# Linear attention and a gated scan: one product moved from GpSimd to VectorE, B and C's products in one piece, eight mask slots

## Chip, cores and metric

One NeuronCore of a Trainium2 chip. The metric is the device time of one execution in microseconds, the median of several runs.

## What is computed

The input `x` has 128 sequences of 64 steps and 256 features. Two blocks follow one another, in float32:

```
xn = layernorm(x);  q, k, v = xn @ Wq + bq, xn @ Wk + bk, xn @ Wv + bv    # 16 heads of 16
k, v masked;  q = softmax(q over a head), k = softmax(k over the steps)
y = q @ (k^T v) per head
x1 = x + silu(layernorm(y) * (1 + scale) + shift) @ film_out_W + b        # scale, shift from cond

h = (layernorm(x1) * (1 + scale) + shift)[:, perm]                        # scale, shift, gate from cond
xm, z = split(h @ W_in);  xm = silu(causal conv of 4 taps(xm) + conv_b)   # 512 channels
dtr, B, C = split(xm @ W_xp);  dt = softplus(dtr @ W_dt + b_dt)           # 64, 16, 16 columns
step: hst = hst * exp(dt * A) + (dt * x) B;  y = hst . C                  # 512 channels x 16 states
out = x1 + gate * ((y + xm * D) * silu(z)) @ W_out, put back by inverse perm
```

## The kernel before

**Attention** runs over 64 tiles of 128 rows (two sequences) in a software pipeline of 11 stages. Each engine goes through iterations j = 0 to 73 and does, in an order written out by hand, its part of every stage; tile k is in stage s at iteration k + s. Semaphores count tiles. SyncE's queue (lines 1115 to 1182) does in iteration j: `load(j+2)` of an input tile into ten slots, `load_mask(j+2)`, which spreads one row of the mask over 128 partitions into one of MRING = 4 slots `mneg`, then the store of the normalised `xh` of tile j-10 to DRAM, then the store of `x1` of tile j-7. `reuse(sp, S["k_biased"], k, MRING)` makes the mask load of tile k wait until VectorE has biased the keys of tile k - MRING (line 1607, which reads `mneg`). Everything in SyncE's queue is issued in order. GpSimd's iteration (line 1207) begins with `xh` of tile j-9, which waits until `xh` of tile j-11 is stored (two slots; SyncE issues that store in its iteration j-1), then scales `kT`, adds a bias to `xt`, computes three `rstd`, and normalises `yn`. TensorE turns `yn` (1337), then `xn` (1342), then projects (1352), and makes the keys (1370), which VectorE biases.

**The scan** goes over 16 chunks of T = 4 steps. The time is the batch's: a tile is 128 sequences at one step by 512 channels. A body of 64 items (one item is one of 16 states at one step) is written per chunk, `slot(c, i)` on each engine, with the side work of the next two chunks put into fixed slots (tables at lines 310 to 324: a position counts slots from the body of chunk k - 2). Per item:

- ScalarE makes four pieces of exp(dt A), `decay` (832), two pieces per slot, a block of eight items ahead;
- TensorE turns them into one of four PSUM banks (708), two slots ahead. It may do so once the item four before has been updated;
- VectorE multiplies the bank with the state, `keep_state` (970), and adds dt x times B, `feed_state` (980). It goes by pairs of items, `two_slots` (1011): two products, two updates;
- GpSimd or, for the items in ON_SCALAR, ScalarE scales the new state by C into one of eight slots (616, 878). For the ten items in PAIRED GpSimd also adds the scaled state of the item before to it (621), so that TensorE sums one in place of two;
- TensorE adds it up by transposing products (723), five slots later.

Side work per chunk: modulation of gathered rows on GpSimd, transposes `h`, input products `u` and `z` (two slots each), the taps of the convolution, whose last one ScalarE makes from its own SBUF copy `raw` (868) and whose other three GpSimd multiplies and adds (636, 640) in slots 46 to 69; `dtr`, then B and C's product `bcT` in two pieces of two column groups in slots 20 and 21 (775), their reduction `bc`, four `dt` products (785). ScalarE's softplus reads them twice, Relu and Abs (860, 861), then Exp (873) and one Ln (908, slot 36). GpSimd adds dt in slots 39, 41, 43, 45 (647) and multiplies it by x in slots 40, 42, 44, 46 (650). TensorE turns the products in slots 57, 59 and 66, 69 (789) and ScalarE copies them to `dtx`. Output products `out0` stand in slots 60, 61, 63, `out1` in slots 9 to 11 (753). For the first chunk VectorE does the sums and products itself (1078, 1081), and the pieces of a product stand back to back.

At the end a last stretch adds rows to the residual and stores them.

Of the kernel before, what the change touches and what calls it, by code (L numbers as in the profile page):

```python
# [25 lines left out]
P = 128  # L26
# [20 lines left out]
ON_SCALAR = (1, 3, 5, 16, 26, 36, 45, 47, 49, 51, 53, 55, 57, 59, 61, 63)  # L47
PAIRED = (7, 11, 13, 21, 23, 25, 29, 31, 33, 35)
RING = 8
# [3 lines left out]
AHEAD = 2  # L53
MRING = 4
STAGES = 11
# [9 lines left out]
def build(nc, x, cond, itok, mask, norm_scale, norm_bias, Wq, bq, Wk, bk, Wv, bv,  # L65
# [11 lines left out]
    with ExitStack() as ctx:  # L77
# [192 lines left out]
        s_tapadd = sem("conv_taps_added_gpsimd")  # L270
        s_tap0 = sem("conv_first_tap")
        s_xs, s_zs = sem("xs_ready"), sem("zs_ready")
# [33 lines left out]
        def at(start, *slots):  # L306
# [3 lines left out]
        SLOTS = {"dtr": at(B1, 13, 14), "out1": at(B3, 9, 10, 11), "dt0": at(B1, 18), "z0": at(B1, 16, 17),  # L310
                 "bcT": at(B1, 20, 21), "dt1": at(B1, 23), "bc": at(B1, 24, 25), "z1": at(B1, 28, 29),
                 "dt2": at(B1, 27), "z2": at(B1, 32, 33), "dt3": at(B1, 31), "z3": at(B1, 35, 36),
# [9 lines left out]
        MODULATE, CARRY, LN = at(0, 14, 18), B1 + 9, B1 + 36  # L322
        SOFTPLUS = at(B1, *range(39, 39 + 2 * CB))
        ROWS = {"out1": B3 + 12, "out0": B3 + 0}
# [259 lines left out]
        def mamba_gpsimd(gp):  # L584
# [39 lines left out]
            def add_tap(k, which, step):  # L624

                m, j = POOL_TAPS[which]
                if (m, j) not in taps_of(k):
                    return
                done = taps_to(k) + taps_of(k).index((m, j))
                x = xs[k % 2][:, m, :]  # L630
                if step == 0:
                    if j == 0:
                        gp.wait_ge(s_tap0, k * CB + m + 1)
                    reached(gp, s_tapadd, done)
                    apart(gp)
                    gp.tensor_scalar(tap[:, :], raw[:, m, j * P:j * P + TOK], taps[:, m, j:j + 1], 1.0,  # L636
                                     ALU.mult, ALU.mult).then_inc(s_tapmul, 1)
                else:
                    gp.wait_ge(s_tapmul, done + 1 - len(POOL_TAPS))
                    gp.tensor_tensor(x, x, tap[:, :], ALU.add).then_inc(s_tapadd, 1)  # L640

            def softplus_times_x(k, m, step):

                v = dtT[k % 2][:, m, :]
                if step == 0:
                    gp.wait_ge(s_softexp, softplus_steps(k + 1))
                    gp.tensor_tensor(v, v, tmp[:, m, :], ALU.add).then_inc(s_dt, 1)
                else:
                    gp.wait_ge(s_dt, k * CB + m + 1)
                    gp.tensor_tensor(tmp[:, m, :], v, xs[k % 2][:, m, :], ALU.mult).then_inc(s_dtxT, 1)  # L650

# [7 lines left out]
            def slot(c, i):  # L659

                if scanned(c) and i not in on_scalar_of(c):
                    scale_state(c, i)
                if scanned(c) and i - 1 in paired_of(c):
                    add_pair(c, i - 1)
                for n in range(STAGES_IN):
                    if c == CHUNKS - 1 and i == EARLY_SLOTS[n]:
                        add_early(n)
                for step, position in enumerate(POOL_TAP_SLOTS):
                    k = chunk_at(c, i, position)
                    if k is not None:  # L670
                        add_tap(k, step // 2, step % 2)
                k = chunk_at(c, i, CARRY)
                if k is not None:
                    carry(k)
                for step, position in enumerate(MODULATE):
                    k = chunk_at(c, i, position)
                    if k is not None:
                        modulate(k, step)
                for step, position in enumerate(SOFTPLUS):
                    k = chunk_at(c, i, position)  # L680
                    if k is not None:
                        softplus_times_x(k, step // 2, step % 2)

# [11 lines left out]
        def mamba_tensor(pe):  # L695
# [43 lines left out]
            def fill(k, job, piece):  # L739
# [33 lines left out]
                elif kind == "bcT":  # L773
                    for g in (2 * piece, 2 * piece + 1):
                        mm = pe.matmul(side[g * 2 * DS:(g + 1) * 2 * DS, :], w_xp[:, g, DTR:DTR + 2 * DS],
# [47 lines left out]
        def mamba_scalar(act):  # L823
# [11 lines left out]
            def move(k, job):  # L835
# [8 lines left out]
                elif kind == "u":  # L844
                    if k == 1:
                        act.wait_ge(s_carry0, b + 1)
                    elif b == 0:
                        act.wait_ge(s_carried, max(k, 1))
                    ins = act.activation(raw[:, b, (TAPS - 1) * P:], side[:, :], ACT.Copy)
                elif kind == "dtr":  # L850
# [6 lines left out]
                elif kind == "dt":  # L857
                    if b == 0:
                        reached(act, s_decay, (k - 1) * BLOCKS * GROUP * CB)
                    act.activation(dtT[k % 2][:, b, :], side[:, :], ACT.Relu, bias=dt_bias[:, b:b + 1])  # L860
                    ins = act.activation(tmp[:, b, :], side[:, :], ACT.Abs, bias=dt_bias[:, b:b + 1])
                ins.then_inc(s_side_moved[side_turn(k, job)[0]], 1)
                if kind == "u":

                    moved(act, k, job)
                    if b == 0:
                        reached(act, s_skip, (k - 1) * T)
                    act.activation(xs[k % 2][:, b, :], raw[:, b, (TAPS - 1) * P:], ACT.Identity,
                                   scale=taps[:, b, TAPS - 1:TAPS], bias=conv_bias[:, b:b + 1]).then_inc(s_tap0, 1)
                if kind == "dt":  # L870

                    moved(act, k, job)
                    act.activation(tmp[:, b, :], tmp[:, b, :], ACT.Exp, scale=-1.0).then_inc(s_softexp, 1)
# [86 lines left out]
        def mamba_vector(ve):  # L960
# [44 lines left out]
            def copy_x(k, t):  # L1005
# [3 lines left out]
                    .then_inc(s_side_moved[side_turn(k, f"x{t}")[0]], 1)  # L1009

            def two_slots(c, i):

# [11 lines left out]
                if (c, i) == (0, 0):  # L1024
                    copy_x(0, 1)
                for s in (i, i + 1):
                    for job in ROWS:
# [16 lines left out]
            def first_taps(k, m, s_added):  # L1044

                x = xs[k][:, m, :]
                ve.wait_ge(s_tap0, k * CB + m + 1)
                for j in range(TAPS - 1):
# [10 lines left out]
            def first_move(k, job):  # L1059
# [5 lines left out]
                else:  # L1065
                    ve.wait_ge(s_carry0, b + 1)
                    ve.tensor_copy(raw[:, b, (TAPS - 1) * P:], side[:, :])\
                        .then_inc(s_side_moved[side_turn(k, job)[0]], 1)
                    moved(ve, k, job)
                    ve.tensor_scalar(xs[k][:, b, :], raw[:, b, (TAPS - 1) * P:], taps[:, b, TAPS - 1:TAPS],  # L1070
                                     conv_bias[:, b:b + 1], ALU.mult, ALU.add).then_inc(s_tap0, 1)

            def first_softplus():
# [5 lines left out]
                for m in range(CB):  # L1079
                    ve.wait_ge(s_dt, m + 1)  # L1080
                    ve.tensor_tensor(tmp[:, m, :], dtT[0][:, m, :], xs[0][:, m, :], ALU.mult).then_inc(s_dtxT, 1)

# [634 lines left out]
```

## Time and profile before

| | us |
|---|---|
| median of 3 runs | 1968.82 (1967.66 to 1969.59) |
| profiled execution, its own time | 1967.15 |
| its span, first to last instruction | 1965.2 |
| TensorE busy | 1834.1 (93%) |
| VectorE busy | 1803.8 (92%) |
| ScalarE busy | 1732.2 (88%) |
| GpSimd busy | 1659.0 (84%) |

A matmul of TensorE is pipelined, and its busy time counts overlaps of ends that are modelled. Attention takes some 460 us, the first chunk's preparation some 50, the scan 1420, the last rows 33. "Idle before" in a row is the idle time of the engine just before the instruction, with what released it.

### The profile page before, as it was taken

The numbers are of one execution on the slowest core, as the hardware profiler recorded it, in microseconds if no ns is written. First come the engines' busy times: TensorE is split into PE (matmuls) and PEld (weight loads), VectorE is DVE, ScalarE is ACT, GpSimd is POOL, SyncE is SP. The second block draws the span as 40 slices with busy tenths as digits, with TensorE's granted clock in tenths as the row PEclk, the third lists the DMA queues.
The fourth block names the chain that finished last, engine by engine and source line by source line (L and its number), as shares of the span: only waits on it lengthen the run. The fifth ranks groups of instructions, "written<-read, shape, count | busy, mean of one in ns | idle before, by whom it ended". The sixth has DMA issues, their size and how long they took to land. (4 is left out here: it accounts for less than half of the span.)

```text
span 1965.2 us, 43163 instructions
## 1 busy us (share of the span) xinstructions
PE 1834.1 (93%) x12641; PEld 1426.2 (73%) x12641; DVE 1803.8 (92%) x3561; ACT 1732.2 (88%) x4073; POOL 1659.0 (84%) x1867
## 2 busy tenths in 40 slices
PE   6999999996899999999999999999999999999973
PEld 4666666663578878787878888787878888787873
DVE  4999999994899999999999999999999999999997
ACT  3777777773999999999999999999999999999981
POOL 3677777785689999999999999999999999998681
PEclk8999999998999999999999999999999999999997
DMA  6122222212000000000000000000000000001274
GB/s 173 54 76 73 71 76 67 77 56 75 1 12 12 12 12 18 7 17 18 12 12 12 12 12 17 7 18 18 12 12 12 12 12 12 12 7 50 66 230 182
DMA packets 71482, 80.82 MB, mean 41 GB/s; under 512 B 12243, under 2 KB 63699, under 8 KB 69204
## 3 DMA queue, kind: packets, MB, share of 16 engines
q1 hardware_dynamic: 69024, 70.67, 11.4%
q10 hardware_dynamic: 2228, 7.41, 1.0%
q8 instruction: 105, 1.72, 0.4%
q14 instruction: 125, 1.02, 0.2%
HBM read 44.46 MB, written 33.59 MB: 40 GB/s over the span
## 5 line engine op out<-in xcount | busy, mean ns | idle before, releaser
L832 ACT ACTIVATE decay<-dtT,decay_rate 128x256 f32<-128x256 f32 x2048 | 870.9, 498 | 0.5
L708 PE MATMUL bank<-ident,decay 128*128 128x128 f32 x4096 | 612.6, 273 | 30.3 <-DVE state L980 12.6
L723 PEld LDWEIGHTS bank<-ident,scaled 128*128 128x128 f32 x3496 | 414.5, 141 | 182.2 <-issue 136.1
L708 PEld LDWEIGHTS bank<-ident,decay 128*128 128x128 f32 x4096 | 478.5, 142 | 87.9 <-issue 47.0
L723 PE MATMUL bank<-ident,scaled 128*128 128x128 f32 x3496 | 529.6, 274 | 1.1 <-POOL scaled L616 0.2
L970 DVE TENSOR_TENSOR bank<-bank,fresh 128x512 f32<-128x512 f32 x512 | 336.8, 689 | 32.7 <-PE bank L708 31.6
L970 DVE TENSOR_TENSOR bank<-bank,state 128x512 f32<-128x512 f32 x512 | 337.1, 690 | 24.3 <-PE bank L708 24.3
L980 DVE SCALAR_TENSOR_TENSOR fresh<-dtx,bc,bank 128x512 f32<-128x512 f32 x512 | 356.9, 737 | 0.0
L980 DVE SCALAR_TENSOR_TENSOR state<-dtx,bc,bank 128x512 f32<-128x512 f32 x512 | 356.9, 737 | 0.0
L616 POOL TENSOR_SCALAR scaled<-state,bc 128x512 f32<-128x512 f32 x378 | 260.0, 694 | 63.8 <-DVE state L980 39.2
L616 POOL TENSOR_SCALAR scaled<-fresh,bc 128x512 f32<-128x512 f32 x381 | 263.6, 694 | 34.7 <-DVE fresh L980 22.4
L640 POOL TENSOR_TENSOR xs<-xs,tap_bcT 128x512 f32<-128x512 f32 x174 | 222.5, 1279 | 13.3
L621 POOL TENSOR_TENSOR scaled<-scaled 128x512 f32<-128x512 f32 x150 | 192.1, 1281 | 2.5
L1429 ACT ACTIVATE kT<-kT,kmax_neg 128x64 f32<-128x64 f32 x256 | 85.9, 336 | 75.3 <-DVE kmax_neg L1620 75.3
L636 POOL TENSOR_SCALAR tap_bcT<-raw,taps 128x512 f32<-128x512 f32 x174 | 120.7, 694 | 24.1 <-DVE xs L1070 23.7
L753 PE MATMUL bank<-w_out,zs 128*128 128x256 f32 x512 | 127.6, 382 | 1.1 <-DVE zs L989 0.9
L1204 POOL TENSOR_SCALAR xh<-x,mv,rstd 128x256 f32<-128x256 f32 x64 | 78.1, 1220 | 56.0 <-issue 53.9
L765 PE MATMUL bank<-hT,w_in 128*128 128x512 f32 x240 | 122.3, 595 | 1.8 <-ACT hT L843 1.3
L1301 PE MATMUL bank<-w_qv,xnT 128*128 128x512 f32 x256 | 123.7, 606 | 0.0
L756 PE MATMUL bank<-hT,w_in 128*128 128x512 f32 x240 | 122.8, 594 | 0.0
L878 ACT ACTIVATE scaled<-state,bc 128x512 f32<-128x512 f32 x134 | 95.8, 715 | 11.6 <-DVE state L980 11.5
L1204 POOL TENSOR_SCALAR yn<-yt,mv,rstd 128x256 f32<-128x256 f32 x64 | 91.4, 1428 | 15.2 <-POOL rstd L1235 15.2
(164 smaller groups left out, 3172.2 us busy)
## 6 DMA issues: line engine op xcount, KB each, us to landing
xt<-in_x_dram SPq DMA_DIRECT2D x64, 128.0 KB, 2.6
resid<-x SPq DMA_DIRECT2D x64, 128.0 KB, 2.6
normed<-xh SPq DMA_DIRECT2D x64, 128.0 KB, 2.8
fin_r<-resid SPq DMA_DIRECT2D x8, 1024.0 KB, 4.9
xg<-normed SPq DMA_DIRECT2D x60, 128.0 KB, 2.1
ssm_out<-yo SPq DMA_DIRECT2D x30, 256.0 KB, 2.0
tap_bcT<-ssm_out SPq DMA_DIRECT2D x44, 128.0 KB, 2.3
mneg<-mask_rows SPq DMA_DIRECT2D x64, 64.0 KB, 2.8
```

The source lines that it names most:

```text
L616: gp.tensor_scalar(dst, h, cn, 1.0, ALU.mult, ALU.mult).then_inc(s_scaled_p, 1)
L621: gp.tensor_tensor(scaled[:, i % RING, :], scaled[:, i % RING, :], scaled[:, (i - 1) % RING, :], ALU.add)\
L640: gp.tensor_tensor(x, x, tap[:, :], ALU.add).then_inc(s_tapadd, 1)
L708: mm = pe.transpose(dec_bank[i % DECAY_BANKS][:, m * P:(m + 1) * P], decay[:, i // BLOCK % 2, n % GROUP, m, t % HALF * P:(t % HALF + 1) * ...
L723: mm = pe.matmul(y_bank[t % HALF][:, m * P:(m + 1) * P], scaled[:, i % RING, m * P:(m + 1) * P], ident[:, :], is_transpose=True, start=Fal ...
L753: mm = pe.matmul(side[:, q * D:(q + 1) * D], zs[k % 2][:, m, t * P:(t + 1) * P], w_out[:, m, :], start=(m == 0), stop=(m == CB - 1))
L756: mm = pe.matmul(side[:, :], w_in[:, piece, DI + b * P:DI + (b + 1) * P], hidden(k)[:, piece, :], start=(piece == 0), stop=(piece == FB - 1))
L832: act.activation(decay[:, block % 2, e // CB, m, :], dtT[c % 2][:, m, half * HTOK:(half + 1) * HTOK], ACT.Exp, scale=decay_rate[:, m, n:n ...
L970: ve.tensor_tensor(dec_bank[i % DECAY_BANKS][:, :], dec_bank[i % DECAY_BANKS][:, :], h, ALU.mult)\
L980: ve.scalar_tensor_tensor(state_of(n, t), dtx[c % 2][:, t, :], bc[:, c % 2, t, n:n + 1], dec_bank[i % DECAY_BANKS][:, :], ALU.mult, ALU.ad ...
L1204: gp.tensor_scalar(dst, src, mv[:, norm, slot, 0:1], rstd[:, norm, slot, 0:1], ALU.subtract, ALU.mult).then_inc(S[done], 1)
L1301: mm = pe.matmul(b_qvp[:, :], xnT[:, k % 2, c, :], w_qv[:, c, :], start=(c == 0), stop=(c == FB - 1))
```

## The change

The product dt times x of chunks 1 to 15 goes from GpSimd (650) to VectorE, as `times_x` after the updates of slots 46, 48, 50 and 52. PAIRED gets items 39, 41 and 43. `bcT` is one piece of four column groups in slot 20, and its copy goes from slot 23 to 22. The last tap is read from PSUM right after the copy `raw`, ahead of the signal that frees the bank; GpSimd's first tap waits for that signal. The softplus makes Abs first, then Relu, and Exp waits for Abs alone. MRING is 8.

```diff
-PAIRED = (7, 11, 13, 21, 23, 25, 29, 31, 33, 35)
+PAIRED = (7, 11, 13, 21, 23, 25, 29, 31, 33, 35, 39, 41, 43)
-MRING = 4
+MRING = 8
...
-                 "bcT": at(B1, 20, 21), "dt1": at(B1, 23), "bc": at(B1, 24, 25), "z1": at(B1, 28, 29),
+                 "bcT": at(B1, 20), "dt1": at(B1, 23), "bc": at(B1, 24, 25), "z1": at(B1, 28, 29),
...
-        SOFTPLUS = at(B1, *range(39, 39 + 2 * CB))
+        SOFTPLUS, TIMES_X = at(B1, 39, 41, 43, 45), at(B1, 46, 48, 50, 52)
...
-                        gp.wait_ge(s_tap0, k * CB + m + 1)
+                        moved(gp, k, f"u{m}")
...
-            def softplus_times_x(k, m, step):
+            def softplus_sum(k, m):
 
                 v = dtT[k % 2][:, m, :]
-                if step == 0:
-                    gp.wait_ge(s_softexp, softplus_steps(k + 1))
-                    gp.tensor_tensor(v, v, tmp[:, m, :], ALU.add).then_inc(s_dt, 1)
-                else:
-                    gp.wait_ge(s_dt, k * CB + m + 1)
-                    gp.tensor_tensor(tmp[:, m, :], v, xs[k % 2][:, m, :], ALU.mult).then_inc(s_dtxT, 1)
+                gp.wait_ge(s_softexp, softplus_steps(k + 1))
+                gp.tensor_tensor(v, v, tmp[:, m, :], ALU.add).then_inc(s_dt, 1)
...
-                    for g in (2 * piece, 2 * piece + 1):
+                    for g in range(CB):
...
-                    ins = act.activation(raw[:, b, (TAPS - 1) * P:], side[:, :], ACT.Copy)
+                    act.activation(raw[:, b, (TAPS - 1) * P:], side[:, :], ACT.Copy)
+                    if b == 0:
+                        reached(act, s_skip, (k - 1) * T)
+                    ins = act.activation(xs[k % 2][:, b, :], side[:, :], ACT.Identity,
+                                         scale=taps[:, b, TAPS - 1:TAPS], bias=conv_bias[:, b:b + 1])
...
-                    act.activation(dtT[k % 2][:, b, :], side[:, :], ACT.Relu, bias=dt_bias[:, b:b + 1])
-                    ins = act.activation(tmp[:, b, :], side[:, :], ACT.Abs, bias=dt_bias[:, b:b + 1])
+                    act.activation(tmp[:, b, :], side[:, :], ACT.Abs, bias=dt_bias[:, b:b + 1]).then_inc(s_abs, 1)
+                    ins = act.activation(dtT[k % 2][:, b, :], side[:, :], ACT.Relu, bias=dt_bias[:, b:b + 1])
                 ins.then_inc(s_side_moved[side_turn(k, job)[0]], 1)
-                if kind == "u":
-
-                    moved(act, k, job)
-                    if b == 0:
-                        reached(act, s_skip, (k - 1) * T)
-                    act.activation(xs[k % 2][:, b, :], raw[:, b, (TAPS - 1) * P:], ACT.Identity,
-                                   scale=taps[:, b, TAPS - 1:TAPS], bias=conv_bias[:, b:b + 1]).then_inc(s_tap0, 1)
                 if kind == "dt":
-
-                    moved(act, k, job)
+                    act.wait_ge(s_abs, k * CB + b + 1)
                     act.activation(tmp[:, b, :], tmp[:, b, :], ACT.Exp, scale=-1.0).then_inc(s_softexp, 1)
...
+            def times_x(k, m):
+
+                ve.wait_ge(s_dt, k * CB + m + 1)
+                ve.tensor_tensor(tmp[:, m, :], dtT[k % 2][:, m, :], xs[k % 2][:, m, :], ALU.mult).then_inc(s_dtxT, 1)
...
+                for m, position in enumerate(TIMES_X):
+                    k = chunk_at(c, i, position)
+                    if k is not None:
+                        times_x(k, m)
```

VectorE's own moves of `u2` and `u3` of chunk 1 ahead of the scan are changed in the same way as ScalarE's.

## Rows read from the trace of the kernel before

**Rows 1.** table of stretches: us, then busy (instructions) of each engine, clock, DMA.

```profile
90.00:430.00 340.00, 314.60 (x2103) 215.26 (x2102) 311.97 (x1054) 263.92 (x948) 268.35 (x317) 1.00 0.23 71
1133.80:1222.80 89.00, 88.51 (x627) 71.55 (x626) 85.16 (x135) 87.49 (x183) 84.10 (x94) 1.00 0.04 13
1164.40:1189.00 24.60, 24.60 (x163) 17.96 (x162) 23.15 (x37) 24.25 (x52) 22.07 (x26) 1.00 0.00 1
```

**Rows 2.** timeline of VectorE in one scan body: start, us, line, count, idle before.

```profile
1131.61 0.70 DVE L970 TENSOR_TENSOR bank<-bank,fresh 128x512 f32<-128x512 f32 x1 [0.84 <-PE bank L708]
...
1193.96 1.28 DVE L970 TENSOR_TENSOR bank<-bank,state 128x512 f32<-128x512 f32 x2
...
1196.47 1.29 DVE L970 TENSOR_TENSOR bank<-bank,fresh 128x512 f32<-128x512 f32 x2
...
1220.60 0.70 DVE L970 TENSOR_TENSOR bank<-bank,fresh 128x512 f32<-128x512 f32 x1 [0.83 <-PE bank L708]
```

**Rows 3.** waits of the same scan body: total, times, longest.

```profile
DVE bank L970 <- PE bank L708: 3.9, 11, 0.8
```

**Rows 4.** VectorE's sums and products ahead of the scan, by source line.

```profile
L1078 DVE TENSOR_TENSOR dtT<-dtT,tmp x4: 676/678/1565, 505.6 to 508.2; 128x512 f32<-128x512 f32 x4
L1081 DVE TENSOR_TENSOR tmp<-dtT,xs x4: 677/677/677, 508.8 to 510.7; 128x512 f32<-128x512 f32 x4
```

**Rows 5.** timeline ahead of the scan, GpSimd and VectorE.

```profile
505.25 1.32 POOL L640 TENSOR_TENSOR xs<-xs,tap_bcT 128x512 f32<-128x512 f32 x1
...
508.85 2.48 DVE L1081 TENSOR_TENSOR tmp<-dtT,xs 128x512 f32<-128x512 f32 x4
```

**Rows 6.** timeline of GpSimd in the scan body.

```profile
1203.24 1.29 POOL L647 TENSOR_TENSOR dtT<-dtT,tmp 128x512 f32<-128x512 f32 x1
...
1211.02 0.69 POOL L616 TENSOR_SCALAR scaled<-fresh,bc 128x512 f32<-128x512 f32 x1
...
1213.72 0.69 POOL L616 TENSOR_SCALAR scaled<-state,bc 128x512 f32<-128x512 f32 x1
```

**Rows 7.** timelines of TensorE: B and C ahead of the scan, then in the body.

```profile
499.32 1.07 PE L775 MATMUL bank<-xs,w_xp 128*32 128x512 f32 x8
...
1166.46 0.14 PEld L775 LDWEIGHTS bank<-xs,w_xp 128*32 128x32 f32 x4 [0.17 <-issue]
1167.44 0.42 PEld L723 LDWEIGHTS bank<-ident,scaled 128*128 128x128 f32 x4 [0.84 <-issue]
```

**Rows 8.** timelines of VectorE and TensorE's loads around item 56.

```profile
1207.72 1.39 DVE L980 SCALAR_TENSOR_TENSOR state<-dtx,bc,bank 128x512 f32<-128x512 f32 x2
...
1211.55 1.29 DVE L970 TENSOR_TENSOR bank<-bank,state 128x512 f32<-128x512 f32 x2
...
1209.46 0.47 PEld L708 LDWEIGHTS bank<-ident,decay 128*128 128x128 f32 x4
```

**Rows 9.** timeline of one attention iteration, all engines and SyncE's queue.

```profile
304.03 0.32 SPq L1127 DMA_DIRECT2D mneg<-mask_rows  x1
...
304.45 0.37 SPq L1167 DMA_DIRECT2D normed<-xh  x1
...
307.47 1.22 POOL L1204 TENSOR_SCALAR xh<-x,mv,rstd 128x256 f32<-128x256 f32 x1 [1.02 <-issue]
...
309.87 0.61 DVE L1607 SCALAR_TENSOR_TENSOR kT<-bank,col,mneg 128x128 f32<-128x128 f32 x2 [0.56 <-PE bank L1370]
...
313.12 0.20 PEld L1337 LDWEIGHTS bank<-ident,yn 128*128 128x128 f32 x2 [0.78 <-issue]
```

**Rows 10.** groups by line in attention, 90 to 430 us: busy, mean, idle before.

```profile
L1607 DVE SCALAR_TENSOR_TENSOR kT<-bank,col,mneg 128x128 f32<-128x128 f32 x106 | 32.3, 346 | 25.2 <-PE bank L1370 25.1
...
L1204 POOL TENSOR_SCALAR xh<-x,mv,rstd 128x256 f32<-128x256 f32 x53 | 64.6, 1220 | 53.1 <-issue 51.8 <-DMA normed<-xh 1.3
```

**Rows 11.** VectorE's two-input product in attention, by source line.

```profile
L1625 DVE SCALAR_TENSOR_TENSOR fs<-fth,fu x64: 408/415/620, 50.5 to 454.5; 128x256 f32<-128x256 f32 x64
```

**Rows 12.** GpSimd's pair additions in the scan body.

```profile
L621 POOL TENSOR_TENSOR scaled<-scaled 128x512 f32<-128x512 f32 x10 | 12.8, 1284 | 0.2
```

More of the change, by code:

```diff
@@ L270, in build @@
         s_tapadd = sem("conv_taps_added_gpsimd")
-        s_tap0 = sem("conv_first_tap")
+        s_abs = sem("softplus_abs")
         s_xs, s_zs = sem("xs_ready"), sem("zs_ready")
@@ L678, in slot @@
                         modulate(k, step)
-                for step, position in enumerate(SOFTPLUS):
+                for m, position in enumerate(SOFTPLUS):
                     k = chunk_at(c, i, position)
                     if k is not None:
-                        softplus_times_x(k, step // 2, step % 2)
+                        softplus_sum(k, m)
             gp.wait_ge(s_modulated, modulations(1))
@@ L1046, in first_taps @@
                 x = xs[k][:, m, :]
-                ve.wait_ge(s_tap0, k * CB + m + 1)
+                moved(ve, k, f"u{m}")
                 for j in range(TAPS - 1):
@@ L1066, in first_move @@
                     ve.wait_ge(s_carry0, b + 1)
-                    ve.tensor_copy(raw[:, b, (TAPS - 1) * P:], side[:, :])\
+                    ve.tensor_copy(raw[:, b, (TAPS - 1) * P:], side[:, :])
+                    ve.tensor_scalar(xs[k][:, b, :], side[:, :], taps[:, b, TAPS - 1:TAPS],
+                                     conv_bias[:, b:b + 1], ALU.mult, ALU.add)\
                         .then_inc(s_side_moved[side_turn(k, job)[0]], 1)
-                    moved(ve, k, job)
-                    ve.tensor_scalar(xs[k][:, b, :], raw[:, b, (TAPS - 1) * P:], taps[:, b, TAPS - 1:TAPS],
-                                     conv_bias[:, b:b + 1], ALU.mult, ALU.add).then_inc(s_tap0, 1)
             def first_softplus():
@@ L1079, in first_softplus @@
                 for m in range(CB):
-                    ve.wait_ge(s_dt, m + 1)
-                    ve.tensor_tensor(tmp[:, m, :], dtT[0][:, m, :], xs[0][:, m, :], ALU.mult).then_inc(s_dtxT, 1)
+                    times_x(0, m)
             first_modulation()
```

## Prediction

> **What bounds the kernel now.** I read the table of stretches first, for attention and for one scan body [rows 1]. In the body (89.0 us, 64 items) four engines are each busy 84 to 88.5 us, so no share says which one sets the pace; in attention VectorE has 312.0 of 340 us. What paces each stage has to be read from waits in the order of time. VectorE's timeline in the scan shows pairs of products and pairs of updates, 2.51 us for two items, back to back [rows 2]. 64 items are 80.3 us; four gates and two scalings of output rows, some 0.60 each, bring 83.9. A body repeats after 88.99 us (two equal waits of 0.84 and 0.83 [rows 2]), so VectorE idles 5.1 us per body; 3.9 of it is seen as waits for decays turned by TensorE [rows 3]. Those waits lie in items 13 to 39 and at items 63, 0 and 1. Items 40 to 62 have none. From 1164.4 to 1189.0 (items 22 to 39) TensorE is busy without a gap and VectorE idles 1.45 us [rows 1]: there TensorE sets the pace.
>
> In attention VectorE waits 25.1 us over 53 iterations for TensorE's key product, and GpSimd waits 51.8 us before `xh` for nothing that the view names [rows 10]. The timeline of an iteration names it [rows 9]. SyncE issues the mask load at 304.03, which had stood behind VectorE's key biasing, and only then the store of an `xh` that GpSimd had ready more than an iteration before, at 304.45. GpSimd's next `xh` goes into that slot, needs it stored, and starts at 307.47, after 1.02 us of waiting. GpSimd's `yn` is late in turn, TensorE waits 0.78 us at 313.12, and the key product that VectorE wants at 309.30 comes at 309.87. It is a loop through SyncE's queue.
>
> **Part 1: eight slots of mask rows.** The load of tile j+2 waits for the mask of tile j-6 in place of j-2. The wait in SyncE's queue goes; the loads themselves, 64 of 64 KB, stay. The store of `xh` then goes out as soon as `xh` is done, the 1.02 us go, and `yn` comes up to 1.0 us earlier, more than TensorE's 0.78. What is late next is VectorE itself: an iteration of 6.5 us less its 0.5 of waiting is 6.0, and GpSimd's 5.1 to 5.3 us of work fit in. Bounds: 0 (another link of the same length) to 25.1 us plus some 4 before 90 us. I take 24, near the top, because the rows show each link.
>
> **Part 2: dt times x on VectorE.** 60 instructions leave GpSimd (two-input ones take 1284 ns [rows 12]) and 60 come to VectorE, four per body in 15 bodies, in slots 46, 48, 50 and 52. The same product runs four times before the scan: 2.48 us for four, 677 ns long, 0.60 from start to start [rows 4, 5]. That is 2.40 us per body, and it lies in items 46 to 53, where VectorE has no idle time: all of it moves the end, 36.0 us. Queued behind each are the next two products, and behind those everything. The new wait for the sum `dt` costs nothing: the last of GpSimd's four sums starts at 1203.24 [rows 6] and is done at 1204.5, and VectorE's product that reads it would come after item 53's update, at 1209.0 or later. The transposes that read the product stand in slots 57 and 59, four slots later.
>
> Then there is the port. The scan's other VectorE work has one input in PSUM; this has both in SBUF. One row shows what that does beside GpSimd: the first of the four sums takes 1565 ns, not 678, having started 0.30 us into a two-input addition of GpSimd that ends 1.02 us later [rows 4, 5]. The price, 0.89 us, is that of one unlucky arrival. A free arrival costs 0. In slots 46 to 53 GpSimd works without a break on a cycle of 2.70 us (1211.02 to 1213.72 [rows 6]) with one two-input addition of 1.28 us: arrivals at random meet it in 47% of cases and wait 0.6 us, so 0.28 on average. Beside a one-input instruction the rows show little: `fs` in attention reads two SBUF tiles, is mostly beside a running `yn`, and takes 415 ns in the median and 620 at worst [rows 11]. I take 0.28 per product, 1.12 per body, 17 us in all; bounds 0 and 0.89 each (0 and 53 us).
>
> The Trainium skill ("SBUF — State Buffer", "SBUF: two separate sides") says that a VectorE instruction with two SBUF inputs and a GpSimd one that reads SBUF take an exclusive lock for the whole instruction and the loser fully blocks. By that rule the one-input instructions block too; its time is among the rivals.
>
> **Part 3: thirteen pairs.** Three more additions on GpSimd (1284 ns [rows 12]) against four products fewer: 3.9 - 5.1 = -1.3 us per body. VectorE's products hold GpSimd up by as much as 2.4. Its 84.1 of 89.0 us [rows 1] become at most 85.2, no bound. TensorE makes three sums of four products fewer (0.47 us each, as the four loads of [rows 8]) in slots 43 to 47. It is busy there and falls behind: item 56's decay may be turned once item 52 is updated, at 1208.46, and is begun at 1209.46, 2.1 us ahead of the product that reads it [rows 8]. Behind it stand the output product and two transposes, more than the lead covers, and VectorE waits 0.83 us at item 63 [rows 2] and again at 0 and 1. The sums saved, or VectorE's own delay, let TensorE start item 56 when it may, 1.0 us earlier less 0.1 for the signal. Either would do, so they don't add up. Bounds 0 and 1.3; I take 0.90 per body, 13.5 us in all.
>
> **Part 4: B and C's products at once.** Now two pieces in slots 20 and 21, each 0.98 us of TensorE until the next load (1166.46 to 1167.44) and some 0.1 more ahead of it. Before the scan the two pieces happen to stand back to back, and all eight records take 1.07 us [rows 7]: four column groups run at once. So a piece is free, 1.07 us. From there to item 39 TensorE has no gap and VectorE idles 1.45 us [rows 1], so all of it reaches the end: 1.07 per body, 16 us. Bounds 0 and 1.07. ScalarE (87.5 of 89 us busy [rows 1]) is close behind.
>
> **Part 5: first tap and absolute value.** ScalarE reads the first tap from PSUM without waiting for its own copy, and the exponential follows the absolute value after one instruction, so some 0.1 us goes at each of eight places per body. ScalarE is no bound: 0. The side bank is held 0.7 us longer, against four slots until its next use: 0. Ahead of the scan, where this chain is exposed, I take -0.5 us (bounds 0 and -2).
>
> **Sum.** Per body +2.40 + 1.12 - 0.90 - 1.07 = +1.55; 15 bodies +23.3. Attention -24.0, ahead of the scan -0.5. In all -1.2 us on the profiled execution's 1967.15, so 1965.9. The median of the runs stands 1.67 above it, and 1968.82 - 1.2 gives **1967.6 us**. Two large terms cancel. 0.2% (4 us) is about what a measurement of this kernel tells from no change.
>
> **Rivals.**
> A, the forecast, chance 0.42. With the port at 0 to 0.6 us and attention at -15 to -29 its own range is 1955 to 1985; it lies below 1964.9 in 0.16, within 0.2% in 0.18, above in 0.08.
> B, faster, 0.25: GpSimd has caught up by slot 46, VectorE gets the port first, and attention gives 29. 15 x (2.40 - 1.97) = 6.5, less 29.5: 1946. For it: VectorE's delay lets GpSimd catch up. Against: GpSimd has no gap when the first product comes.
> C, slower, 0.15: VectorE waits out whatever GpSimd runs. On a cycle of 1.28, 0.69 and 0.69 us within 2.70 the mean rest is (1.64 + 0.48 + 0.48) / 5.4 = 0.48 us: 15 x (2.40 + 1.93 - 1.97) = 35, less 24.5, gives 1980; with the 0.89 of the one row each time, 2004. It decides from about 0.37 us a product, where the sum passes +4. For it: the 1565 ns. Against: `fs`. It is what the skill's lock would do.
> D, slower, 0.10: the mask ring wins nothing, since another wait of 1 us stands behind it. 23.3 - 0.5 is +22.8: 1992.
> E, slower, 0.08: TensorE's savings don't reach VectorE because ScalarE's decays are late then. -1.2 + 15 x 1.97 is +28: 1997.
> The range reaches from just below B's point to E's, **1944 to 1996**, and leaves out a part of B, of C and of E. Faster: B and 0.16 of A, 0.41; same 0.18; slower: C, D, E and 0.08 of A, 0.41.
>
> **What would show it.** Attention: `xh` without its 1.0 us of waiting, VectorE's 25 us before the key biasing under 4, iterations of 6.0 us. Scan: bodies of 90.5 us; four products per body, mean 0.9 us, some near 0.68 and some over 1.2; the wait at item 63 under 0.2; waits at items 25, 27 and 35 gone; B and C's eight records in 1.07 us. I am wrong if a body is over 92 or under 89.5, or if attention's iterations stay at 6.5.

## The result and the profile after

The changed kernel takes 1995.70 us (median of four runs, 1993.66 to 1997.47), the one before 1969.20; the ratio is 1.0136, interval 1.0118 to 1.0153. It is slower by 26.5 us (forecast: 1.2 us faster), at the upper edge of the range. The profiled execution took 1997.47 us, its span is 1995.8 (before 1965.2): 30.6 us to account for. I take them from the starts of VectorE's chunks: attention, from the first `qe` to the last, went from 413.0 to 399.8 us; from there to the scan's first item it went from 76.3 to 78.4; fifteen bodies of the scan from 1331.6 to 1373.8 (+42.2). The rest is equal within 0.5 us.

The table of stretches, as [rows 1], for attention and one scan body:

```profile
90.00:430.00 340.00, 321.80 (x2170) 221.05 (x2168) 315.85 (x1081) 269.04 (x970) 290.40 (x328) 1.00 0.25 72
1140.00:1231.80 91.80, 86.91 (x615) 69.87 (x614) 89.93 (x140) 87.21 (x183) 84.98 (x93) 1.00 0.04 13
```

A body takes 91.80 us, not 90.5; VectorE is busy in 89.9 of it. I call GpSimd's scalings and taps, which read one tile (0.69 us), one-input instructions, and its additions (1.28 us) two-input ones; "the product" is dt times x on VectorE (line 1006). Its groups and waits in that body, beside [rows 3, 12]:

```profile
L1006 DVE TENSOR_TENSOR tmp<-dtT,xs 128x512 f32<-128x512 f32 x4 | 5.7, 1422 | 0.0
L621 POOL TENSOR_TENSOR scaled<-scaled 128x512 f32<-128x512 f32 x13 | 16.7, 1282 | 0.2
...
DVE bank L962 <- PE bank L704: 1.8, 4, 0.6
```

Waits for TensorE fell from 3.9 to 1.8 us, and the four products take 5.7. The timeline (start, us) shows which of the four is long, GpSimd first, then VectorE:

```profile
1195.90 1.36 POOL L616 TENSOR_SCALAR scaled<-state,bc 128x512 f32<-128x512 f32 x2 [1.43 <-DVE state L972]
1197.23 1.28 POOL L646 TENSOR_TENSOR dtT<-dtT,tmp 128x512 f32<-128x512 f32 x1
...
1204.89 1.29 POOL L646 TENSOR_TENSOR dtT<-dtT,tmp 128x512 f32<-128x512 f32 x1
1206.14 0.71 POOL L616 TENSOR_SCALAR scaled<-state,bc 128x512 f32<-128x512 f32 x1
1206.80 1.28 POOL L621 TENSOR_TENSOR scaled<-scaled 128x512 f32<-128x512 f32 x1
1208.03 1.28 POOL L646 TENSOR_TENSOR dtT<-dtT,tmp 128x512 f32<-128x512 f32 x1
1209.28 1.15 POOL L616 TENSOR_SCALAR scaled<-state,bc 128x512 f32<-128x512 f32 x1
...
1206.30 3.57 DVE L1006 TENSOR_TENSOR tmp<-dtT,xs 128x512 f32<-128x512 f32 x1
1209.79 1.29 DVE L962 TENSOR_TENSOR bank<-bank,state 128x512 f32<-128x512 f32 x2
```

The first product arrives 0.16 us into a one-input instruction of GpSimd and stays through it and two two-input ones. It ends 0.56 us behind the second, its own work, and GpSimd's next one-input instruction takes 1.15 instead of 0.69. Its input was complete long before: it needs the first of four sums (at 1197.23), the third is the one at 1204.89. In fourteen of fifteen bodies it is so; in the one where the product arrives at the end of a sum, it takes 0.69 and the body 89.36. The other three take 0.70 to 0.72 in most bodies. In those fourteen the product arrives 10.4 us behind GpSimd's last wait for a state of VectorE (1195.90), so the two engines keep the same distance from body to body.

In attention the ring's wait is gone, and another has come (groups, 90 to 430 us, as [rows 10]; then VectorE's and GpSimd's timelines):

```profile
L1225 POOL TENSOR_TENSOR xt<-xt,b_fo 128x256 f32<-128x256 f32 x53 | 54.1, 1020 | 0.0
L1217 POOL TENSOR_TENSOR kT<-kT,krec 128x256 f32<-128x256 f32 x54 | 33.1, 614 | 30.7 <-DVE krec L1659 29.7
...
L1606 DVE SCALAR_TENSOR_TENSOR kT<-bank,col,mneg 128x128 f32<-128x128 f32 x106 | 32.3, 346 | 22.1 <-PE bank L1369 19.2
```

```profile
306.27 0.61 DVE L1606 SCALAR_TENSOR_TENSOR kT<-bank,col,mneg 128x128 f32<-128x128 f32 x2 [0.76 <-PE bank L1369]
...
298.39 0.61 POOL L1217 TENSOR_TENSOR kT<-kT,krec 128x256 f32<-128x256 f32 x1 [1.08 <-DVE krec L1659]
298.97 1.03 POOL L1225 TENSOR_TENSOR xt<-xt,b_fo 128x256 f32<-128x256 f32 x1
...
301.41 1.44 POOL L1203 TENSOR_SCALAR yn<-yt,mv,rstd 128x256 f32<-128x256 f32 x1 [0.24 <-POOL rstd L1234]
```

`xh` has no wait. The iterations alternate, 6.57 and 5.91 us: in one of two GpSimd waits 1.08 us for `krec`, its `yn` ends at 302.85, TensorE gets to the key product late, and VectorE waits 0.76. (That each step of this chain sets the next one is read from the times; `nobias` below tests one of them.)

### The profile page after: what moved, and what is told of

It is laid out like the page before. It is cut to its first block and busy times, and to the rows that moved or that the text cites. A ratio compares the mean times of both kernels' runs of the same rounds, so it can differ in the third digit from the quotient of the medians.

```text
span 1995.8 us, 42834 instructions
## 1 busy us (share of the span) xinstructions
PE 1817.4 (91%) x12461; PEld 1412.5 (71%) x12461; DVE 1870.0 (94%) x3621; ACT 1723.2 (86%) x4073; POOL 1684.5 (84%) x1852
## 3 DMA queue, kind: packets, MB, share of 16 engines
q14 instruction: 125, 1.02, 0.2%
## 5 line engine op out<-in xcount | busy, mean ns | idle before, releaser
L704 PE MATMUL bank<-ident,decay 128*128 128x128 f32 x4096 | 620.4, 276 | 74.7 <-DVE fresh L972 39.0
L719 PEld LDWEIGHTS bank<-ident,scaled 128*128 128x128 f32 x3316 | 400.1, 143 | 172.8 <-issue 117.0
L719 PE MATMUL bank<-ident,scaled 128*128 128x128 f32 x3316 | 506.9, 276 | 13.6 <-POOL scaled L621 13.6
L616 POOL TENSOR_SCALAR scaled<-state,bc 128x512 f32<-128x512 f32 x378 | 274.7, 731 | 81.1 <-DVE state L972 73.5
L962 DVE TENSOR_TENSOR bank<-bank,state 128x512 f32<-128x512 f32 x512 | 332.8, 689 | 7.9 <-PE bank L704 7.8
L616 POOL TENSOR_SCALAR scaled<-fresh,bc 128x512 f32<-128x512 f32 x381 | 277.5, 730 | 47.6 <-DVE fresh L972 33.8
L621 POOL TENSOR_TENSOR scaled<-scaled 128x512 f32<-128x512 f32 x195 | 249.9, 1281 | 2.5
L870 ACT ACTIVATE scaled<-fresh,bc 128x512 f32<-128x512 f32 x131 | 94.2, 719 | 40.1 <-DVE fresh L972 39.8
```

The costliest lines, as they stand in the source:

```text
L616: gp.tensor_scalar(dst, h, cn, 1.0, ALU.mult, ALU.mult).then_inc(s_scaled_p, 1)
L621: gp.tensor_tensor(scaled[:, i % RING, :], scaled[:, i % RING, :], scaled[:, (i - 1) % RING, :], ALU.add)\
L704: mm = pe.transpose(dec_bank[i % DECAY_BANKS][:, m * P:(m + 1) * P], decay[:, i // BLOCK % 2, n % GROUP, m, t % HALF * P:(t % HALF + 1) * ...
L719: mm = pe.matmul(y_bank[t % HALF][:, m * P:(m + 1) * P], scaled[:, i % RING, m * P:(m + 1) * P], ident[:, :], is_transpose=True, start=Fal ...
L870: act.activation(dst, h, ACT.Copy, scale=cn).then_inc(s_scaled_a, 1)
L962: ve.tensor_tensor(dec_bank[i % DECAY_BANKS][:, :], dec_bank[i % DECAY_BANKS][:, :], h, ALU.mult)\
```

## The experiments

"Bodies" are the time from one body's first item to the next one's. A gap of VectorE is here what the time from start to start has above the usual one of back-to-back instructions (0.60 us for a product, 0.66 for an update); this is some 0.1 us more than the idle time that a row shows.

**Each part alone.** Edits on the kernel before:

```
mring:  MRING = 4                ->  MRING = 8
bct:    "bcT": at(B1, 20, 21)    ->  at(B1, 20);   for g in range(CB)
pairs:  PAIRED = (..., 33, 35)   ->  (..., 33, 35, 39, 41, 43)
timesx: SOFTPLUS at 39, 41, 43, 45; TIMES_X at 46, 48, 50, 52 on VectorE
```

> The kernel before with eight slots of mask rows and nothing else. In the changed kernel attention's iterations took 6.57 and 5.91 us in turn (mean 6.24, before 6.44). Theory M: that gain is the ring's own and nothing later eats it, so this kernel is 13 us faster than the one before (1956), with the same two periods in turn, and the scan's bodies stay at 89.0. Rival: other parts slow attention or the stretch behind it (it became 2.1 us longer in the changed kernel), and the ring alone gives the forecast 24: 1945. Second rival: the stretch ahead of the scan grows here too, and the gain is 11.

Measured: 1954.99, ratio 0.9932 (0.9916 to 0.9949), 6.57 and 5.91 us in turn, bodies of 89.0. Theory M holds.

> The kernel before with B and C's products in one piece and nothing else. Theory: of the 2.4 us of VectorE's waiting that went per body in the changed kernel, 1.07 is this part's (waits at items 25 and 27 smaller): bodies of 87.9, 16 us faster, 1953. Rival: TensorE's freed 1.07 us is taken by ScalarE's lateness and bodies stay within 0.2 of 89.0: 1966 to 1969.

Measured: 1956.00, ratio 0.9932 (0.9915 to 0.9948), bodies of 88.0 and 88.5 in turn: the theory, with 13.4 us for its 16. VectorE's gaps at items 23 to 35 fell by 1.1 us per body, as forecast; that at item 63 grew from 0.93 to 1.28 on average. A third was given back there.

> The kernel before with thirteen pairs in place of ten and nothing else; GpSimd keeps dt times x. Theory: TensorE's lead at items 52 to 63 comes back and the waits at items 63, 0 and 1 (1.45 us per body) fall below 0.5: bodies of 88.0 to 88.1, 13.5 us faster, 1955. Rival: GpSimd, with 3.9 us more per body on 84 to 86 of 89, delivers its sums late, TensorE waits for them, and bodies take 89.5 to 91: 1975 to 1995.

Measured: 2023.81, ratio 1.0279 (1.0262 to 1.0296), bodies of 92.5 on average. The rival, and more than it said: TensorE waits 5.3 us for GpSimd's pair additions. Waits of one body:

```profile
DVE bank L970 <- PE bank L708: 6.9, 12, 2.2
PEld bank L723 <- POOL scaled L621: 5.3, 3, 3.5
```

> The kernel before with dt times x on VectorE (slots 46, 48, 50, 52) and nothing else; ten pairs. Theory P (port): what the forecast missed in the scan is one product per body that waits out GpSimd's instructions one after another (3.57 us in the changed kernel, the other three 0.70 to 0.72). Here the waits at items 63, 0 and 1 (1.45) go and those up to 39 stay, so a body is 89.0 + 2.4 + 3.0 - 1.4 = 93.0 and the time 2029; the four products' sum is 4.5 to 6 us per body. Rival: the long wait belongs to thirteen pairs (a GpSimd that is later), the products here take 0.9 on average, and bodies are 91.2 to 91.8: 2001 to 2010.

Measured: 1996.05, ratio 1.0140 (1.0123 to 1.0156), bodies of 90.76. Theory P falls; it is the rival's side, and below it: all four products take 0.88 us, and the waits at items 63, 0 and 1 are gone. The long wait needs more than the move of the product.

**The changed kernel with one thing undone or moved.**

```
a10:   PAIRED without 39, 41, 43
late:  TIMES_X = at(B1, 46, 48, 50, 52)  ->  at(B1, 48, 50, 52, 54)
sum47: SOFTPLUS = at(B1, 39, 41, 43, 45) ->  at(B1, 39, 41, 43, 47)
```

> The changed kernel with ten pairs again (39, 41 and 43 taken out). Theory P13: the product that waits out several GpSimd instructions belongs to the three new pairs, which put two two-input additions in a row where the first product arrives. With ten pairs the four products take 0.88 us each as in the kernel with dt times x alone, bodies are 90.0 to 90.3, and the time is 1968 to 1972. Rival: it is the one-piece product of B and C or the mask ring that shifted the arrival; the first product stays at 3.5 us and the time is above 1985.

Measured: 1965.62, ratio 0.9983 (0.9971 to 0.9994), bodies of 89.64, all products 0.88 us. Theory P13, with a body and a time a little below its ranges. VectorE's gaps are 2.46 us per body, with thirteen pairs 2.47: the three pairs won no wait and cost 30 us. GpSimd, then VectorE:

```profile
1192.77 0.69 POOL L616 TENSOR_SCALAR scaled<-state,bc 128x512 f32<-128x512 f32 x1 [0.35 <-DVE state L972]
1193.43 1.13 POOL L636 TENSOR_SCALAR tap_bcT<-raw,taps 128x512 f32<-128x512 f32 x1
...
1193.11 0.89 DVE L1006 TENSOR_TENSOR tmp<-dtT,xs 128x512 f32<-128x512 f32 x1
1193.92 1.28 DVE L962 TENSOR_TENSOR bank<-bank,state 128x512 f32<-128x512 f32 x2
```

GpSimd started on the state that VectorE had just updated, so the product arrives 0.34 us into that instruction. It is the same distance in all fifteen bodies: no chance is in it.

> The changed kernel with VectorE's four products one pair of items later (slots 48, 50, 52, 54). Theory: what a product waits for is decided by what GpSimd runs when it arrives and what comes next there. In the changed kernel's trace it would arrive some 0.55 us before the end of GpSimd's last sum, with a one-input instruction next, and that gives way: first product 1.2 us, the others 0.7, bodies of 89.4 to 89.7 as the one body of the changed kernel whose first product took 0.69 (89.36), time 1958 to 1965. Rival: VectorE's wait is the same 3 us wherever the product stands, as GpSimd is never idle there: 1993 to 1998.

Measured: 1960.09, ratio 0.9962 (0.9948 to 0.9976), bodies of 89.27, first product 1.05: as the theory says, to within 0.15 us. The same work, one pair of items later, takes 35.6 us less than the changed kernel. The first product arrives 0.80 us into a sum:

```profile
1190.21 1.29 POOL L646 TENSOR_TENSOR dtT<-dtT,tmp 128x512 f32<-128x512 f32 x1
1191.46 1.15 POOL L616 TENSOR_SCALAR scaled<-state,bc 128x512 f32<-128x512 f32 x1
...
1191.01 1.05 DVE L1006 TENSOR_TENSOR tmp<-dtT,xs 128x512 f32<-128x512 f32 x1
```

> The changed kernel with GpSimd's fourth sum of dt in slot 47 in place of 45, so that after the pair addition the first product stands beside, GpSimd runs a one-input instruction. Theory N (the next instruction decides): the product gives way to two-input instructions only; it now waits out one (the pair) and takes 2.3 us in place of 3.57, bodies 90.5. Rival R (the trials of the last set: a product always goes next): the 3.57 us then were no wait for the port, and the product still takes over 3 us or ends at the same place relative to the fourth sum, which it may be waiting for.

Measured: 1976.98 (one run), bodies of 90.50, first product 2.33 us in fourteen of fifteen. Theory N's number. The wait is one for GpSimd: an addition that was moved away took 1.2 us of it along.

```profile
1197.14 1.28 POOL L621 TENSOR_TENSOR scaled<-scaled 128x512 f32<-128x512 f32 x1
1198.39 1.15 POOL L616 TENSOR_SCALAR scaled<-state,bc 128x512 f32<-128x512 f32 x1
...
1196.65 2.33 DVE L1006 TENSOR_TENSOR tmp<-dtT,xs 128x512 f32<-128x512 f32 x1
```

**The port by itself.** Behind the kernel's end, both engines run on tiles of their own (128 x 512):

```
gp: six instructions back to back, each .then_inc(s_probe_p, 1)
ve: wait_ge(s_probe_p, first of the six); one instruction
```

> The kernel before with twenty short trials behind its end: VectorE and GpSimd work on tiles of their own, 128 x 512, and VectorE's instruction is released by the end of the first of six back-to-back GpSimd instructions, so it arrives some 0.1 us into the second. Adds some 100 us of its own; its output is the kernel's. Theory T: a VectorE product of two SBUF tiles waits out the running GpSimd instruction whatever it is, then goes ahead of a one-input instruction and behind a two-input one. So: alone 0.68 us; six one-input: 1.2 to 1.3; six two-input: over 6 (all that are left); two two-input then one-input: 1.8; two one-input then two-input: over 5; one, one, two, two, one, one: 3.7. With a PSUM tile as one input, or one SBUF tile alone, 0.7 in all cases. Rival L (lottery by turn): after the running instruction the product always goes next, 1.2 to 1.3 behind one-input and 1.8 behind two-input instructions, and the 3.57 us had another cause.

Measured (each trial twice). Beside a two-input instruction the product took 1.73 us whatever came next. Where it lost to a running one-input instruction it took 1.17, with a two-input one next as with a one-input one; where both began within some 0.06 us it could also go first (0.69) and GpSimd's instruction took 1.23. Theory T falls, Rival L holds. With one input in PSUM nothing waited (0.70). A VectorE instruction with one SBUF tile alone (a scaling, SBUF to SBUF) waited too: it took 1.47 beside two-input and 0.91 beside one-input instructions. Here the product beside two-input additions, then the one with a PSUM input:

```profile
1964.52 6.58 POOL L251 TENSOR_TENSOR decay<-scaled 128x512 f32<-128x512 f32 x5 [0.15 <-POOL decay L253]
...
1965.82 1.73 DVE L265 TENSOR_TENSOR scaled<-scaled 128x512 f32<-128x512 f32 x1 [4.59 <-POOL decay L251]
...
1992.17 0.70 DVE L267 TENSOR_TENSOR bank<-bank,scaled 128x512 f32<-128x512 f32 x1 [5.12 <-POOL decay L251]
```

The Trainium skill ("SBUF — State Buffer", "SBUF: two separate sides") has this as an exclusive lock for the whole instruction; the trials and the four products of 0.88 agree, one-input GpSimd instructions included. From that rule I expected the rest of one instruction, and the scan shows three. Attention does not agree with it. VectorE's `fs` reads two SBUF tiles, and in the changed kernel it mostly begins inside GpSimd's running `yn`:

```profile
307.17 1.23 POOL L1203 TENSOR_SCALAR yn<-yt,mv,rstd 128x256 f32<-128x256 f32 x1 [0.24 <-POOL rstd L1234]
...
307.72 0.41 DVE L1624 SCALAR_TENSOR_TENSOR fs<-fth,fu 128x256 f32<-128x256 f32 x1
```

In all 27 cases where it begins 0.47 to 0.86 us into `yn`, it takes 0.42 and `yn` its 1.23: neither waits. So the record of a GpSimd instruction is not always time in which VectorE is kept out. In the kernel before, `fs` often began 0.03 to 0.12 us into `yn`: it took its 0.42 there, and `yn` 1.47 us or more in place of 1.23, so the one that waited was GpSimd. My reading of `fs` looked at VectorE's side alone, and it did not carry over to the scan's scalings.

> The kernel before with thirty trials behind its end. In each VectorE runs what it runs in the scan, two products from PSUM, two updates, then a product of two SBUF tiles, beside ten back-to-back GpSimd instructions on other tiles; the first product's width (64 to 512 columns) moves the last one's arrival over 0.5 us. GpSimd's kinds in order (2 two-input, 1 one-input): 2121221121 (as in the changed kernel's scan), 2121111111, 2222222222; each without waits of its own and with satisfied ones and the small semaphore instructions. Theory N: in the first pattern the product that arrives in the third one-input... instruction, with two two-input ones next, takes over 3 us; in the second never over 1.3. Theory R (always next): no product takes more than 2.0 us in any pattern. If only the style with waits shows 3 us, GpSimd's queue decides.

> The kernel before with twenty-five trials behind its end, GpSimd always 2121221121, VectorE as in the last trials, the last product arriving 0.05 to 0.21 us into the one-input instruction that two two-input ones follow (in the scan it arrives 0.14 to 0.19 into it). Five conditions: as before; GpSimd's additions in place (I); the product on the scan's own tiles (R); ScalarE copying from and to SBUF beside it (A); all three and TensorE streaming from SBUF (IRAT). Theory O (the other engines or the in-place form turn the order at the port): only the conditions with that letter show the 3 us of the scan. Rival W (the instant of arrival does): all conditions show it for the arrivals between 0.14 and 0.19. If no trial is over 2 us, what gives GpSimd's two-input instruction the port in the scan stays open.

In the first of the two sets VectorE's pair of products and pair of updates stood ahead of the measured product; in the second the conditions were added (`dst` as input of GpSimd's addition, `dtT` and `xs` as inputs of the product, copies on ScalarE, products on TensorE). Measured: none of the 55 trials took over 1.80 us. With arrival at 0.16 us into the one-input instruction the product took 1.07 to 1.08 in all five conditions of the second set. Theories N, O and W fall for isolated instructions.

Three kernels looked for the reason in the scan itself, all edits of the changed one:

```
apartall:  apart(gp) ahead of the pair's and the sum's tensor_tensor
waitmoved: ve.wait_ge(s_dt, ...) ahead of keep_state(c, i), not at the product
sweep:     for q in range(k - 1): ve.memset(pause[:, 4 * q:4 * q + 4], 0.0)
           ahead of chunk k's first product
```

> The changed kernel with the small separate semaphore instruction, which GpSimd has ahead of each one-input instruction, put ahead of its pair additions and sums of dt too. Theory S (GpSimd's queue decides): two GpSimd instructions that follow each other without such an instruction leave the port no gap, and with it the product goes next: 1.1 us in place of 3.57, bodies of 89.4. Rival N (two-input instructions go first whatever stands between): 3.5 us as now, bodies 91.8.

Measured: 1994.58 (one run), bodies of 91.8, first product 3.55, in thirteen of fifteen. Theory S falls.

> The changed kernel with the wait for the sum dt taken from VectorE's product and put two items of work earlier, ahead of the two products with the decays; it is satisfied by then. In the isolated trials the product had no wait of its own, in the scan it has one, and this is the difference left. Theory E (the wait on the instruction): the product then goes ahead of GpSimd's next instruction, 1.1 us in place of 3.57, bodies of 89.4. Rival: 3.5 us and 91.8 as before, and the wait plays no part.

Measured: 1997.38 (one run), bodies of 91.8, first product 3.57, in fourteen of fifteen. Theory E falls.

> The changed kernel with k - 1 tiny fills (128 x 4) ahead of the first product of chunk k, so that in the scan itself the product arrives later by some 0.06 us per fill, 0 to 0.9 us over the fifteen bodies. Theory I (the instant of arrival relative to GpSimd's instructions): the product takes 3.5 us for the early arrivals and 0.7 to 2.4 for later ones, changing in steps where GpSimd's instructions begin. Rival K (the kind of the next instruction, at every boundary): arrivals beside the one-input instruction take 3.5 less the delay, those beside the first two-input one 3.5 less the delay too, since another two-input one is next, and the product always ends 0.57 us behind the fourth sum.

Measured: 1999.11 (one run). A fill took some 0.015 us, so the arrivals moved only from 0.16 to 0.35 us into the one-input instruction. In thirteen of fifteen bodies the product ended 0.55 us behind the fourth sum (3.58 down to 3.37 us): in that stretch the instant does not matter, as Rival K has it. The ninth body says that the kind of the next instruction is not the rule either: there the product stood behind two more, one-input ones, and ended 0.54 us behind the second of them.

```profile
1299.85 1.32 POOL L647 TENSOR_TENSOR dtT<-dtT,tmp 128x512 f32<-128x512 f32 x1
1301.11 0.73 POOL L617 TENSOR_SCALAR scaled<-state,bc 128x512 f32<-128x512 f32 x1
1301.77 0.74 POOL L637 TENSOR_SCALAR tap_bcT<-raw,taps 128x512 f32<-128x512 f32 x1
1302.60 1.57 POOL L641 TENSOR_TENSOR xs<-xs,tap_bcT 128x512 f32<-128x512 f32 x1
...
1298.27 4.78 DVE L1007 TENSOR_TENSOR tmp<-dtT,xs 128x512 f32<-128x512 f32 x1
```

So it is shown that the product waits for GpSimd, how long, and that moving either side moves it. What lets GpSimd's queued instructions go ahead of a waiting VectorE product stays open.

**Attention's next wait**, on the ring alone (the bias is left out of 240 of 256 columns):

```
gp.tensor_tensor(x[:, 0:16], x[:, 0:16], b_fo[:, 0:16], ALU.add)
```

> Eight slots of mask rows alone, and GpSimd's addition of the output bias in attention cut to 16 of 256 columns (the bias is left out of the other 240). With the ring alone the iterations take 6.57 and 5.91 us in turn: in one of two GpSimd waits 1.1 us for VectorE's krec and its yn is then late for TensorE. Theory G: the loop is GpSimd's chain kT, bias, rstd, yn; 0.8 us off it makes yn early in every iteration, VectorE never waits for TensorE's key product, and all iterations take 5.85 to 5.95: 20 us less than the ring alone, 1935. Rival: the loop runs through TensorE and ScalarE, and the iterations stay at 6.2 on average: 1953 to 1957.

Measured: 1949.79 (one run), iterations of 6.33 and 5.92. That is 5 us less than the ring alone, where Theory G has 20. VectorE's wait for the key product fell from 19.2 to 10.0 us, and by the theory it would have gone. GpSimd's chain is part of the loop and not all of it.

**Combinations without the product on VectorE.** combo is mring and bct; back10 is the changed kernel with dt times x on GpSimd and ten pairs.

> The kernel before with eight slots of mask rows and B and C's products in one piece, nothing else (dt times x stays on GpSimd, ten pairs). The single runs gave 14.4 and 13.4 us. Theory: they lie in different stages and add up: 1941 to 1943. Rival: they share a part and give 20 at most: 1949.

Measured: 1945.42, ratio 0.9882 (0.9866 to 0.9899). Between the two: bodies of 88.0 as in bct, and attention ended at 428.0 us where mring's ended at 423.1. The difference is in the first eight iterations, 61.1 against 56.1 us; behind them the periods are 6.57 and 5.91 in both. Both kernels run the same code there, and such starts differ elsewhere too (a10 58.1, the changed kernel 56.4), so it is not a price of the combination; what makes it stays open.

> The changed kernel with dt times x on GpSimd and ten pairs, that is the kernel before with the mask ring, B and C's products in one piece, and the first tap and absolute value changed. Against the kernel with the first two alone (1945.4) it tells what the last is worth. Theory: nothing in the scan, within 2 us: 1943.5 to 1947.5. Rival: the stretch from attention's end to the scan's start, which grew by 2.1 us in the changed kernel, grows with it: 1947 to 1949.

Measured: 1935.05, ratio 0.9827 (0.9805 to 0.9848): 33 us faster than before and the best of all. Neither expectation held: bodies are 87.52 on average, against 88.03, and attention ended at 423.5, without combo's slow start. VectorE's wait at item 63 fell from 1.40 and 1.03 in turn to 0.71, as the timeline of either shows (combo first):

```profile
1118.05 0.70 DVE L970 TENSOR_TENSOR bank<-bank,fresh 128x512 f32<-128x512 f32 x1 [1.40 <-PE bank L708]
```

```profile
1110.43 0.70 DVE L966 TENSOR_TENSOR bank<-bank,fresh 128x512 f32<-128x512 f32 x1 [0.71 <-PE bank L708]
```

## Why the prediction was wrong

The reading of the kernel before held; the sign was lost on two terms, the wait of the products (27.9 us more than forecast) and attention (10.8 us less won).

**Part 2, dt times x.** The 2.40 us per body were right, and all of it moved the end, as the sum of a body below bears out. The failed step is "arrivals at random meet it in 47% of cases and wait 0.6 us". GpSimd waits for what VectorE has just made, so the distance between the two is fixed, and one arrival repeats in nearly every body. With ten pairs it gave 0.21 us four times (0.88 against 0.68 us), 0.83 in place of my 1.12: near by luck, since the wait was beside a one-input instruction, which I had taken to cost little. With the change's thirteen pairs it gave 2.89 (1209.79 - 1206.30 - 0.60) and three times 0.03: 2.98 per body, 27.9 us more than forecast over fifteen. That is 0.74 a product, between rival C's 0.48 and 0.89, but one price and not four: C's mechanism, an instruction waited out whatever its kind, is what the trials show for the scan's instructions; that one product could wait for three in a row I had excluded by taking the rest of one.

**Part 3, thirteen pairs.** I wrote that the sums saved or VectorE's own delay would do, and they don't add up. That was right: the waits at items 63, 0 and 1 go with ten pairs (timesx, a10), and they were 1.47 us of gaps, more than my 0.90 and my bound of 1.3. So the pairs brought nothing, and I should have looked for what they cost: they fill GpSimd where the product arrives (there it waits 0.35 us for VectorE in a10, and not at all with thirteen). Here they are the difference from 1965.62 to 1995.70. Alone, without the products taken off GpSimd, they cost 54 us.

**Part 4, B and C at once.** Right in size where it stands (eight records in 1.07 us, waits at 25, 27 and 35 gone); alone it kept 11 of the 16 us of the bodies.

**Parts 3 and 4 together** took VectorE's gaps from 5.06 to 2.47 us per body, -2.59, where I had -1.97. The body by measured terms: 89.01 + 2.40 + 2.98 - 2.59 = 91.80, as measured; nothing else in it changed.

**Part 1, the ring.** The link was right: `xh` without a wait, and alone 14.4 us. The size was not: 13.2 us of attention in place of 24 (1.6 of them in the first eight iterations, which vary by more between kernels with the same code there). "What is late next is VectorE itself" failed. GpSimd's 5.1 to 5.3 us of work did not fit in as a sum: from one `kT` to the next it takes 5.7 us even without a wait for `krec` (298.39 to 304.10), since it waits for its own `rstd`, and its bias addition takes 1.02 us (0.74 before). That addition now starts 0.05 us ahead of VectorE's `qe`, which takes its usual 0.39; that the one holds up the other is read from these times. With its wait for `krec` GpSimd is late in every second iteration.

**Part 5** I put at nothing in the scan; back10 against combo gives 0.5 us per body, 7.6 in all. Ahead of the scan I had -0.5. The stretch between attention and scan took 76.1 to 76.7 us in six kernels without it, 77.9 in a seventh (nobias), and 76.6 to 78.4 with it. The three longest (the changed kernel 78.4, apartall 78.0, nobias 77.9) are those in which TensorE's granted clock fell for 3.4 us some 10 us into the stretch (table as [rows 1]). TensorE was busy in 9.5 of the 12.9 us before that, and in it without a break:

```profile
432.90:436.30 3.40, 3.40 (x5) 1.34 (x5) 0.70 (x3) 0.00 (x0) 3.08 (x5) 0.51 0.23 77
```

That clock is the lower of its two levels, 1.2 GHz. Of the other kernels, those whose clock stood at 1.00 for the first 20 us of the stretch took 76.1 to 76.3 without Part 5 and 76.6 to 76.9 with it. So some 0.5 of the 2.1 us are Part 5's, against my sign, and some 1.6 go with the clock. In the kernel before, the same products had a granted clock of 1.00.

In sum: 15 x (2.40 + 2.98 - 2.59) = 41.9, and 41.9 - 13.2 + 2.1 = +30.8 by the terms, 30.6 measured, -1.2 forecast. The time came near rival E's (1997) by another road: TensorE's savings did reach VectorE, whose waits for turned decays fell from 3.9 to 1.8 us per body.

## What to carry to other kernels

Before moving an elementwise product with two SBUF inputs to VectorE, look at what GpSimd runs at the very slot where it lands, and at what is queued behind: two engines that feed each other are locked in phase, so the price is no average but one fixed number times the bodies, and one pair of items later most of it may be gone (36 us here). Test the parts of a bundle one by one: three of the five were good for 33 us, and the other two cost 61. Extra work for an engine at 84 of 89 us is not covered because its share has room; alone it cost 54 us.

## What the hardware showed that I had not expected

A VectorE product of two SBUF tiles waits for GpSimd's additions and for its one-input scalings too (1.17 against 0.68 us), and so does a VectorE scaling of one SBUF tile (1.47 beside a two-input addition); with a PSUM tile as an input the product took 0.70 in all four trials. GpSimd waits in turn: 1.13 to 1.15 us for an instruction of 0.69. Beside attention's normalisation `yn`, 0.47 us or more into it, neither waited (0.42 and 1.23 us). In isolation the waiting side always went next; in the scan a product waited out up to five GpSimd instructions (4.78 us).
